# Row tiles of a quantised layer spread over four half steps, projections beside them, on one Trainium2 core

## Chip, cores, metric

One core of a Trainium2 chip. The time is device microseconds of one execution of the whole program. TensorE, VectorE, ScalarE, GpSimd and SyncE (which only issues DMAs here) each run their own instruction stream and meet at semaphores. In the profile's rows they are PE (weight loads: PEld), DVE, ACT, POOL and SP.

## What is computed

Four images of 512 tokens by 256 go through five layers, each (but the first) followed by a layer norm over the residual sum. Cut to what matters:

```
h = tok(x)                          # relu(x W0) * (x W1) -> Wo
h = norm(h + attn0(h))              # 16 heads of 16, window of +-64 keys
h = norm(h + ffn0(h))               # 8-bit activations, ternary weights
h = norm(h + attn1(h))              # causal
h = norm(h + moe(h))                # 8 experts, top 2

def act_quant(x):                   # per row
    scale = 127 / max(|x|)
    return clip(round(x * scale), -128, 127) / scale
g, u = bitlinear(x, w_gate), bitlinear(x, w_up)      # 256 -> 1024
h = relu(g) ** 2 * u
ffn0 = bitlinear(h, w_down)                          # 1024 -> 256
```

## The kernel before

Up to some 700 us the kernel works through attention in half steps (`HALVES`, the numbers `eta`). A unit is one tile of 128 rows for four heads; a half step is two heads of a unit. There are 128 units, so half steps 0 to 255, 32 to an image; image 0 to 3 of the window layer come first, then the same four of the causal layer. In each half step all engines do a fixed list: scores of unit eta/2 on TensorE (L809) and their row maxima on VectorE (`maximum`, L1099); 15 half steps later the turned scores (L832), whose exponent ScalarE takes (L630); every second half step a triangle or band is cut off on GpSimd (`select`, L540 to L548) and, 19 half steps after the scores, the values are multiplied (`values`, L848, with `vaug` as stationary side). Each eight half steps the maxima are split in three bf16 parts, turned and sent as extra rows, and four heads go back to rows.

Between these stand the dense steps. `DENSE` gives for each phase and image the half step of its step 0 and `STEPS` the number of steps; `SCHED` puts step c at half step at + c. Within a half step every engine runs `dense(phase, i, c)` last; TensorE and ScalarE have an `early` part too, before the turned scores. Phases: `tok`; `qkv` (projections; index 0 to 3 window layer, 4 to 7 causal): step 0 turns the rows, steps 1 to 4 each make one part of 128 of the queries or keys (L947), which ScalarE copies twice (L709, L710), and VectorE and GpSimd split in three bf16 parts (L1325, L562, L1320); steps 5, 6 make the values (L956), which ScalarE writes to `vaug` (L718). SyncE then copies the parts to the ring of three blocks `qs`, `ks` (`stack`), where it waits for the last turned scores of the block before in the slot. `o`: output projection, residual, norm. `ffn`: the quantised layer. `gate`, `route`, `send` (L582): the choice of experts and the row scatters from GpSimd.

The quantised layer of image i: steps 0, 1 (`quant`) scale and round the rows, step 3 (`FQT`) turns them behind 12 warm-up matmuls, and the four row tiles follow, tile t at step 3 + 2t (`FIRST_TILE`, `PER_TILE`, `tile_at(c, off)`). For tile t at offset 0 TensorE makes gate and up of the first 512 columns (`quantised_half`, L875), ScalarE takes relu and square of gate (L658, L661), VectorE multiplies with up (`hidden`, L1284) in the same half step; at offset 1 the second 512 columns, then maximum and scale (L1291 to L1300) on VectorE and the scaled rows on ScalarE (L753); at `QUANT` = 2 VectorE rounds (L1307); at `TURN` = 3 TensorE turns behind three warm-up matmuls (L794, L1000) and ScalarE copies (L644); at `DOWN` = 4 the second product (L983) and its sum (L1366); at `STATS` = 5 and `NORM` = 6 the norm.

PSUM: one bank is kept for the values; the other seven go round. `take` gives each use, in the order of TensorE's stream, the bank longest not used, and TensorE waits (`opened`) until the bank's last reader is done. A bank of "up" is read by VectorE in `hidden`. Behind half step 297 come experts and the last norm, which the change does not touch.

Of the kernel before, what the change touches and what calls it, by code (L numbers as in the profile page):

```python
# [7 lines left out]
BF16 = mybir.dt.bfloat16  # L8
# [5 lines left out]
P = 128  # L14
B, S, D = 4, 512, 256
# [39 lines left out]
VW = H * SLOT + 16  # L55
NR = 3
UNITS = 2 * B * NG * NT
TO_ROWS, TO_TURNED, TO_VALUES, TO_BACK, TO_HEADS = 11, 15, 19, 28, 29
# [28 lines left out]
def turned_heads(u, half):  # L87
# [9 lines left out]
    ("tok", 0, -20), ("qkv", 0, -8), ("tok", 1, 0), ("bias", 0, 1), ("bias", 1, 2), ("wq", 0, 4), ("wq", 1, 8),  # L97
    ("wq", 2, 12), ("qkv", 1, 14), ("tok", 2, 22), ("tok", 3, 34), ("qkv", 2, 46), ("o", 0, 54), ("ffn", 0, 60),
    ("qkv", 3, 77), ("o", 1, 85), ("ffn", 1, 91), ("qkv", 4, 108), ("o", 2, 117), ("ffn", 2, 123), ("qkv", 5, 140),
    ("o", 3, 149), ("ffn", 3, 155), ("qkv", 6, 172), ("o", 4, 181), ("gate", 0, 185), ("route", 0, 187), ("send", 0, 196), ("qkv", 7, 204), ("o", 5, 213),  # L100
    ("gate", 1, 217), ("route", 1, 219), ("send", 1, 228), ("o", 6, 245), ("gate", 2, 249), ("route", 2, 251), ("send", 2, 271), ("o", 7, 278), ("gate", 3, 282), ("route", 3, 284), ("send", 3, 293))
STEPS = {"tok": 12, "qkv": 8, "o": 6, "ffn": 16, "gate": 2, "route": 9, "send": 4, "bias": 2, "wq": 4}


FQT, FIRST_TILE, PER_TILE = 3, 3, 2
QUANT, TURN, DOWN, STATS, NORM = 2, 3, 4, 5, 6

# [36 lines left out]


SCHED = {}
for _phase, _i, _at in DENSE:
    for _c in range(STEPS[_phase]):
        SCHED.setdefault(_at + _c, []).append((_phase, _i, _c))
HALVES = range(min(SCHED), max(max(SCHED), 2 * UNITS + TO_HEADS) + 1)  # L150

# [47 lines left out]
def build(nc, xT, w01, wtok, wattn, wo, battn, bvcol, brow, wq0, wdn, wgate, consts, masks, w1, w2, b1, b2, lnrow, out):  # L199
# [3 lines left out]
    with ctx:  # L203
# [118 lines left out]
        with ExitStack() as c2:  # L322
# [99 lines left out]
            with nc.Block() as block:  # L422
# [95 lines left out]
                def _(pool):  # L518
# [10 lines left out]
                    pool.wait_ge(prep_pool, 6)  # L529
                    for i in range(2):  # L530
                        pool.memset(vaug[:, i, :, 0:H * SLOT].rearrange("p t (h s) -> p t h s", s=SLOT)
                                    [:, :, :, DH:DH + 1], 1.0).then_inc(prep_pool, 1)
# [69 lines left out]
                def _(act):  # L602
# [67 lines left out]
                    def dense(phase, i, c):  # L670
# [19 lines left out]
                        if phase == "qkv":  # L690
# [21 lines left out]
                            if c in (5, 6):  # L712
                                k = c - 5
                                key = ("qkv", i, f"v{k}")
                                act.wait_ge(*d_full(key))
                                if i < 2:
                                    act.wait_ge(prep_pool, 8)
                                act.activation(  # L718
                                    vaug[:, i % 2, 2 * k:2 * k + 2, 0:H * SLOT].rearrange(
                                        "p t (h s) -> p t h s", s=SLOT)[:, :, :, 0:DH],  # L720
                                    dense_bank(key).rearrange("p (t h s) -> p t h s", t=2, s=DH),
                                    ACT.Copy).then_inc(d_out(key)[0], 1)
# [14 lines left out]
                        if phase == "ffn":  # L737
# [36 lines left out]
                def _(pe):  # L774
# [61 lines left out]
                    def values(u):  # L836
# [9 lines left out]
                        for j in range(HG):  # L846
                            hd = g % NG * HG + j
                            ins = mm(bank(V_BANK)[32 * j:32 * j + 32, lo:hi],  # L848
                                     vaug[:, s % 2, kt, hd * SLOT:hd * SLOT + 32], p[:, j, :],
                                     start=(kt == 0), stop=(kt == NT - 1), skip_group_check=True,  # L850
                                     tile_position=(0, 32 * j))
# [219 lines left out]
                def _(dve):  # L1071
# [15 lines left out]
                    def maximum(u, half, split):  # L1087
# [7 lines left out]
                        n = 0  # L1095
                        for i, heads in enumerate(score_heads(u, half)):
                            dve.wait_ge(*s_full((u, half, i)))
                            for a, j in enumerate(heads):
                                ins = dve.tensor_tensor_reduce(  # L1099
                                    out=junk[:, AT["s", (u, half, i)][0], a * (hi - lo):(a + 1) * (hi - lo)],  # L1100
                                    in0=score_bank((u, half, i))[:, a * (hi - lo):(a + 1) * (hi - lo)], in1=mask,
# [207 lines left out]
                    def dense(phase, i, c):  # L1309
# [43 lines left out]
                        if phase == "ffn":  # L1353
# [9 lines left out]
                            if t is not None:  # L1363
# [393 lines left out]
```

## Time and profile before

| | us |
|---|---|
| median of 3 runs | 1079.14 (1068.04 to 1080.44) |
| profiled execution | 1079.0 |
| its span, first to last instruction | 1077.1 |
| mean granted TensorE clock | 0.926 of full |

The span is what the profile's rows add up to. "Granted clock" is the share of the full 2.4 GHz that TensorE was given in a stretch.

### The profile page before, as it was taken

The page shows a single profiled execution, that of the slowest core. Times are in us where ns is not written, and L with a number is a line of the kernel's source. Part 1 is how long each engine was busy: PE and PEld are TensorE (multiplying, and loading weights), DVE is VectorE, ACT ScalarE, POOL GpSimd, SP SyncE. Part 2 cuts the span into 40 slices and gives each one's busy share as a digit, 9 for nine tenths or more (in the row PEclk, how much of TensorE's full clock was granted, in tenths as well). Part 3 has the DMA queues.
Part 4 walks back from the last instruction along what each step waited for, and adds up shares of the span by engine and source line. Part 5 has one row for each costly group of instructions (what it writes and reads, how often), then busy time and mean ns, then how long its engine had stood idle before and what let it go on. Part 6 is the DMA issues. An engine that isn't in the chain of part 4 may idle for free. (4 is left out here: it accounts for less than half of the span.)

```text
span 1077.1 us, 14453 instructions
## 1 busy us (share of the span) xinstructions
PE 914.4 (85%) x5031; PEld 561.6 (52%) x5054; DVE 546.3 (51%) x2104; ACT 417.6 (39%) x717; POOL 295.2 (27%) x364
## 2 busy tenths in 40 slices
PE   6897999878879879888987979867999999999940
PEld 3454455534535534434533525344687777777830
DVE  1257434678778678757785767541021112111137
ACT  1315334476475566565635545501311211121003
POOL 5101322413413413301324342335021122112232
PEclk9998999999989999988988988978999999999975
DMA  9882341542253252430564360153142353243242
GB/s 352 146 186 31 32 80 21 60 40 35 27 60 38 32 52 36 48 38 2 60 88 72 38 104 21 57 196 97 40 96 52 118 132 66 77 123 69 25 102 78
DMA packets 57511, 81.49 MB, mean 76 GB/s; under 512 B 6624, under 2 KB 51041, under 8 KB 55008
## 3 DMA queue, kind: packets, MB, share of 16 engines
q1 hardware_dynamic: 49520, 70.48, 32.9%
q0 software_dynamic: 7296, 9.47, 5.2%
q8 instruction: 40, 0.66, 0.3%
q10 hardware_dynamic: 624, 0.63, 0.2%
q14 instruction: 31, 0.25, 0.1%
HBM read 35.37 MB, written 19.68 MB: 51 GB/s over the span
## 5 line engine op out<-in xcount | busy, mean ns | idle before, releaser
L1099 DVE CUSTOM_DVE_ANT_0 junk<-ps,maskb 128x256 bf16<-128x256 f32 (+4 forms) x512 | 206.3, 434 | 96.6 <-PE ps L809 93.2
L630 ACT ACTIVATE probs<-ps 128x512 f32<-128x512 f32 (+1 forms) x304 | 159.2, 550 | 118.5 <-PE ps L832 115.4
L1551 PE MATMUL ps<-dxT,qs 128*128 128x320 f32 x512 | 139.6, 433 | 1.3 <-DVE dxT L1617 1.3
L1563 PE MATMUL ps<-ks,hTe 128*128 128x256 f32 x640 | 139.3, 379 | 0.0
L1587 ACT ACTIVATE hTe<-ps,qs 128x640 f32<-128x640 f32 x64 | 50.8, 794 | 204.6 <-PE ps L1551 204.6
L1563 PEld LDWEIGHTS ps<-ks,hTe 128*128 128x128 f32 x640 | 121.3, 190 | 16.1
L1507 POOL DMA_INDIRECT mixed_rows<-ysb,ids x40 | 61.7, 1543 | 228.8 <-DVE ysb L1637 225.9
L832 PE MATMUL ps<-qs,ks 99*128 99x256 bf16 (+4 forms) x512 | 104.1, 289 | 23.4 <-DVE nmax L1099 13.7
L1551 PEld LDWEIGHTS ps<-dxT,qs 128*128 128x128 f32 x512 | 97.2, 190 | 41.5 <-DVE dxT L1617 1.7
L809 PE MATMUL ps<-ks,qs 96*128 96x256 bf16 (+4 forms) x512 | 106.2, 290 | 11.1 <-DVE nmax L1099 5.4
L848 PE MATMUL ps<-probs,vaug 128*32 128x256 f32 (+4 forms) x1024 | 92.2, 434 | 10.5 <-issue 5.7
L545 POOL TENSOR_SCALAR_AFFINE_SELECT probs<-probs 128x256 f32<-128x256 f32 (+1 forms) x64 | 39.8, 622 | 217.9 <-ACT probs L630 217.8
L809 PEld LDWEIGHTS ps<-ks,qs 96*128 96x128 bf16 x512 | 45.6, 101 | 89.9 <-issue 59.1
L1617 DVE COPY dxT<-ps 128x256 f32<-128x256 f32 x40 | 15.6, 420 | 137.7 <-PE ps L1538 137.7
L540 POOL TENSOR_SCALAR_AFFINE_SELECT probs<-probs 128x512 f32<-128x512 f32 x64 | 40.6, 639 | 154.4 <-ACT probs L630 154.0
L1634 DVE TENSOR_TENSOR ysb<-ps,ks 128x256 f32<-128x256 f32 x40 | 17.0, 424 | 123.4 <-PE ps L1563 123.4
L794 PE MATMUL ps<-maskb,identb 128*128 128x512 bf16 x190 | 62.8, 486 | 11.9 <-DVE posu L1254 4.2
L832 PEld LDWEIGHTS ps<-qs,ks 99*128 99x128 bf16 x512 | 43.7, 100 | 53.5 <-DVE nmax L1099 20.0
L901 PE MATMUL ps<-x_sb,tokw 128*128 128x512 f32 x128 | 64.3, 636 | 7.2 <-DMA tokw<-w 7.2
L947 PE MATMUL ps<-actT,aw 128*128 128x512 f32 x128 | 63.1, 620 | 2.5 <-ACT actT L649 1.6
L794 PEld LDWEIGHTS ps<-maskb,identb 128*128 128x128 bf16 x206 | 22.6, 118 | 47.4 <-issue 26.0
L875 PE MATMUL ps<-qgu,work 128*128 128x512 bf16 x122 | 34.5, 396 | 11.4 <-DVE att L1141 4.0
(183 smaller groups left out, 1242.3 us busy)
## 6 DMA issues: line engine op xcount, KB each, us to landing
qs<-parts SPq DMA_DIRECT2D x96, 128.0 KB, 4.7
ks<-parts SPq DMA_DIRECT2D x96, 128.0 KB, 7.4
qs<-w SPq DMA_DIRECT2D x8, 1024.0 KB
ks<-w SPq DMA_DIRECT2D x8, 1024.0 KB, 4.9
dispatched_rows<-att SPq DMA_DIRECT2D x8, 650.0 KB, 16.9
ks<-dispatched_rows SPq DMA_DIRECT2D x4, 650.0 KB, 7.4
x_sb<-xT SPq DMA_DIRECT2D x8, 256.0 KB, 4.2
mixed_rows<-h SPq DMA_DIRECT2D x4, 512.0 KB
```

The source lines that it names most:

```text
L630: act.activation(probs_of(u)[:, heads[0]:heads[-1] + 1, :], turned_bank((u, half, i))[:, 0:len(heads) * w].rearrange("p (j n) -> p j n", n=w),
L794: mm(o, identb[:, :], maskb[:, 0:S], start=True, stop=True)
L809: ins = mm(o[:, a * (hi - lo):(a + 1) * (hi - lo)], qs[0:KS, r, hd, t * P:(t + 1) * P], ks[0:KS, r, hd, lo:hi], start=True, stop=True)
L832: ins = mm(o[:, a * (hi - lo):(a + 1) * (hi - lo)], ks[0:KM, r, hd, kt * P:(kt + 1) * P], qs[0:KM, r, hd, lo:hi], start=True, stop=True)
L848: ins = mm(bank(V_BANK)[32 * j:32 * j + 32, lo:hi], vaug[:, s % 2, kt, hd * SLOT:hd * SLOT + 32], p[:, j, :], start=(kt == 0), stop=(kt == ...
L901: ins = mm(o, tokw[:, k, col:col + P], x_sb[:, k, :], start=(k == 0), stop=(k == KD - 1))
L947: ins = mm(o, w[:, k, col:col + P], actT[:, k, :], start=(k == 0), stop=(k == KD - 1))
L1099: ins = dve.tensor_tensor_reduce(out=junk[:, AT["s", (u, half, i)][0], a * (hi - lo):(a + 1) * (hi - lo)], in0=score_bank((u, half, i))[:, ...
L1507: pool.indirect_dma_start(out=acc, out_offset=bass.IndirectOffsetOnAxis(ap=ids[:, e, t:t + 1], axis=0), in_=ysb[:, e % 2, t, :], in_offset ...
L1551: ins = mm(bank(2 * (n % 2) + c)[:, 0:HC], w1s[:, e % 2, k, m * P:(m + 1) * P], dxT[:, e % 2, k, c * HC:(c + 1) * HC], start=(k == 0), sto ...
L1563: ins = mm(bank(4 + n % 2)[:, 0:D], hTe[:, e % 2, m, t * P:(t + 1) * P], w2s[:, e % 2, m, :], start=(m == 0), stop=(m == MH - 1))
L1587: act.activation(hTe[:, e % 2, m, :].rearrange("p (a n) -> p a n", a=2), ps[:, 2 * (n % 2):2 * (n % 2) + 2, 0:HC], ACT.Silu, bias=b1s[:, e ...
```

## The change

The quantised layer takes 25 steps instead of 16: a row tile starts every four half steps, and its later parts lie at 4, 6, 7, 8 and 9 instead of 2 to 6. `HIDDEN` = 1 moves both products on VectorE, with maximum and scale, and ScalarE's scaled rows, one half step behind the matmuls and squares that feed them. The projections of images 2 to 7 start earlier (46 to 38, 77 to 66, 108 to 98, 140 to 130, 172 to 162, 204 to 196) and take two half steps a step (`stretched`), so they lie beside the quantised layer of the image before (image 2's beside the last `tok`). Image 2's values would then be written while those of image 0 are read: `vaug` gets a third buffer, with a wait on the values' matmuls from image 3 on. The scratch `junk` of the maxima gives up the slot of the bank that scores never use, to make room.

```diff
-    ("qkv", 3, 77), ("o", 1, 85), ("ffn", 1, 91), ("qkv", 4, 108), ("o", 2, 117), ("ffn", 2, 123), ("qkv", 5, 140),
+    ("qkv", 3, 66), ("o", 1, 85), ("ffn", 1, 91), ("qkv", 4, 98), ("o", 2, 117), ("ffn", 2, 123), ("qkv", 5, 130),
...
-FQT, FIRST_TILE, PER_TILE = 3, 3, 2
-QUANT, TURN, DOWN, STATS, NORM = 2, 3, 4, 5, 6
+FQT, FIRST_TILE, PER_TILE = 3, 3, 4
+HIDDEN = 1
+QUANT, TURN, DOWN, STATS, NORM = 4, 6, 7, 8, 9
...
+def stretched(phase, i, c):
+
+    return 2 * c if phase == 'qkv' and 2 <= i else c
...
-        SCHED.setdefault(_at + _c, []).append((_phase, _i, _c))
+        SCHED.setdefault(_at + stretched(_phase, _i, _c), []).append((_phase, _i, _c))
...
-            vaug = sb2("vaug", [P, 2, NT, VW])
+            vaug = sb2("vaug", [P, NV, NT, VW])
...
-            junk = sb2("junk", [P, BANKS, S], BF16)
+            junk = sb2("junk", [P, BANKS - 1, S], BF16)
...
-                                if i < 2:
-                                    act.wait_ge(prep_pool, 8)
+                                if i < NV:
+                                    act.wait_ge(prep_pool, 6 + NV)
+                                elif k == 0:
+                                    act.wait_ge(pv_mm, NG * NT * (i - NV + 1))
...
-                            t = tile_at(c, 1)
+                            t = tile_at(c, HIDDEN + 1)
                             if t is not None:
                                 act.wait_ge(fh_scaled, NT * i + t + 1)
...
-                            t = tile_at(c, 0)
+                            t = tile_at(c, HIDDEN)
                             if t is not None:
                                 hidden(i, t, 0)
...
-                            t = tile_at(c, 1)
+                            t = tile_at(c, HIDDEN + 1)
                             if t is not None:
                                 hidden(i, t, 1)
                                 hidden_scale(i, t)
```

TensorE in the second image's quantised layer, before, from one tile's warm-up matmuls to the next tile's (`qgu` are the gate and up weights, `qdn` the down weights, `ks,qs` the scores, `qs,ks` the turned ones):

```order
L794 MATMUL ps<-maskb,identb 128x512 x3
L1000 MATMUL ps<-identb,work 128x128 x8
L809 MATMUL ps<-ks,qs 128x256 x2
L832 MATMUL ps<-qs,ks 128x256 x2
L858 MATMUL ps<-cst,oT 128x128 x4
L983 MATMUL ps<-qdn,work 128x256 x8
L875 MATMUL ps<-qgu,work 128x512 x4
L809 MATMUL ps<-ks,qs 128x256 x2
L875 MATMUL ps<-qgu,work 128x512 x4
L832 MATMUL ps<-qs,ks 128x192 x2
L848 MATMUL ps<-probs,vaug 32x256 x4
L794 MATMUL ps<-maskb,identb 128x512 x3
```

All of a tile's work stands between two half steps of attention. After the change (lines are 11 higher), from one gate and up pair on:

```order
L886 MATMUL ps<-qgu,work 128x512 x4
L958 MATMUL ps<-actT,aw 128x512 x2
L820 MATMUL ps<-ks,qs 128x192 x2
L886 MATMUL ps<-qgu,work 128x512 x4
L843 MATMUL ps<-qs,ks 128x192 x2
L859 MATMUL ps<-probs,vaug 32x256 x4
L820 MATMUL ps<-ks,qs 128x192 x2
L843 MATMUL ps<-qs,ks 128x192 x2
L805 MATMUL ps<-maskb,identb 128x512 x3
L1011 MATMUL ps<-identb,work 128x128 x8
L958 MATMUL ps<-actT,aw 128x512 x2
L820 MATMUL ps<-ks,qs 128x192 x2
```

A tile's parts stand in different half steps now, with a projection part (`actT,aw`) in every second.

VectorE at the same place, before, from the rounding of a tile on:

```order
L1307 TENSOR_SCALAR work<-work 128x1024
L1284 TENSOR_TENSOR work<-work,ps 128x512
L1099 ISA junk,nmax<-ps,maskb 128x192
L1099 ISA nmax 128x1
L1126 CAST nparts<-nrest 128x4x4
L1099 ISA junk,nmax<-ps,maskb 128x192
L1099 ISA nmax 128x1
L1129 TENSOR_TENSOR nparts<-nrest,nparts 128x4x4
L1284 TENSOR_TENSOR work<-work,ps 128x512
L1291 TENSOR_REDUCE sm<-work 128x1
```

The rounding is followed at once by the next tile's product, and the second product comes one half step later. After:

```order
L1319 TENSOR_SCALAR work<-work 128x1024
L1160 BN_STATS stat<-att 128x6
L1337 TENSOR_TENSOR proj<-proj,parts 128x512
L1111 ISA junk,nmax<-ps,maskb 128x192
L1111 ISA nmax 128x1
L1111 ISA junk,nmax<-ps,maskb 128x192
L1111 ISA nmax 128x1
L1296 TENSOR_TENSOR work<-work,ps 128x512
```

The product follows a half step of maxima, and a projection's subtraction (L1337) stands between.

GpSimd where the last image's projections stand, before (L582 the row scatters, L540 the selects, L562 the casts of a projection part):

```order
L540 AFFINE_SELECT probs<-probs 128x512
L582 DMA dispatched_rows<-h,posu 5120x260 x4
L540 AFFINE_SELECT probs<-probs 128x4x128 x3
L540 AFFINE_SELECT probs<-probs 128x512
L562 CAST parts<-proj 128x512 x2
L540 AFFINE_SELECT probs<-probs 128x4x128
```

After:

```order
L549 AFFINE_SELECT probs<-probs 128x512
L591 DMA dispatched_rows<-h,posu 5120x260 x4
L549 AFFINE_SELECT probs<-probs 128x4x128
L571 CAST parts<-proj 128x512
L549 AFFINE_SELECT probs<-probs 128x4x128
L571 CAST parts<-proj 128x512
L549 AFFINE_SELECT probs<-probs 128x4x128
```

The casts now follow the scatters after one select instead of four.

## Rows read from the trace of the kernel before

**Rows 1.** Page, part 1: busy us of each engine (share of the span), instructions.
```profile
PE 914.4 (85%) x5031; PEld 561.6 (52%) x5054; DVE 546.3 (51%) x2104; ACT 417.6 (39%) x717; POOL 295.2 (27%) x364
```

**Rows 2.** Busy time by stretch: stretch, length, busy us by engine, granted clock, DMA share, GB/s.
```profile
219.30:246.40 27.10, 20.10 (x156) 10.38 (x158) 20.90 (x65) 19.43 (x31) 4.44 (x8) 1.00 0.23 24
246.40:262.70 16.30, 13.73 (x110) 7.48 (x108) 13.64 (x63) 9.96 (x17) 6.92 (x11) 1.00 0.01 3
279.70:298.70 19.00, 15.17 (x108) 7.92 (x107) 13.98 (x57) 9.46 (x18) 5.51 (x9) 0.91 0.13 23
298.70:329.10 30.40, 23.80 (x166) 12.63 (x166) 23.95 (x79) 19.84 (x31) 5.50 (x9) 0.83 0.40 41
329.10:344.70 15.60, 13.90 (x103) 7.61 (x101) 11.97 (x54) 9.42 (x17) 5.85 (x10) 1.00 0.13 24
344.70:359.40 14.70, 14.60 (x109) 9.84 (x108) 10.25 (x44) 9.59 (x18) 8.99 (x13) 1.00 0.84 85
378.40:409.90 31.50, 23.45 (x166) 11.71 (x166) 25.29 (x80) 19.66 (x31) 5.50 (x9) 0.89 0.38 38
409.90:426.70 16.80, 14.79 (x104) 7.55 (x101) 13.57 (x53) 9.91 (x18) 6.39 (x11) 1.00 0.18 29
564.80:586.90 22.10, 16.68 (x96) 7.41 (x93) 12.28 (x47) 10.52 (x20) 9.95 (x13) 0.85 0.24 63
```

**Rows 3.** The same for the score matmuls (L809) alone, one stretch.
```profile
329.10:344.70 15.60, 2.85 (x16) 1.39 (x17) 1.00 0.13 24
```

**Rows 4.** VectorE in order of time: start, us, instruction, [idle before <-who ended it].
```profile
312.57 0.69 DVE L1284 TENSOR_TENSOR work<-work,ps 128x512 f32<-128x512 f32 x1 [1.14 <-ACT work L661]
313.18 0.42 DVE L1099 CUSTOM_DVE_ANT_0 junk<-ps,maskb 128x256 bf16<-128x256 f32 x1
...
314.26 0.69 DVE L1284 TENSOR_TENSOR work<-work,ps 128x512 f32<-128x512 f32 x1 [0.31 <-ACT work L661]
315.05 1.22 DVE L1291 TENSOR_REDUCE sm<-work 128x1 f32<-128x1024 f32 x1
...
316.86 0.21 DVE L1300 TENSOR_SCALAR sm<-sm 128x1 f32<-128x1 f32 x1
...
318.38 0.69 DVE L1307 TENSOR_SCALAR work<-work 128x1024 bf16<-128x1024 f32 x1 [0.30 <-ACT work L753]
318.99 0.48 DVE L1366 SCALAR_TENSOR_TENSOR att<-ps,sm,h 128x256 f32<-128x256 f32 x1
320.11 0.69 DVE L1284 TENSOR_TENSOR work<-work,ps 128x512 f32<-128x512 f32 x1 [0.64 <-ACT work L661]
```

**Rows 5.** What L1284 waited for in the whole span: us, times.
```profile
  ACT work L661: 26.5, 20
```

**Rows 6.** Fill of the values' buffers on GpSimd, and their first writer on ScalarE.
```profile
15.88 2.02 POOL L528 MEMSET vaug<- 128x2304 f32 x1
...
42.06 0.60 ACT L718 ACTIVATE vaug<-ps 128x512 f32<-128x512 f32 x1
```

**Rows 7.** Groups by shape, 53 to 700 us: count | busy us, mean ns | idle before.
```profile
L947 PE MATMUL ps<-actT,aw 128*128 128x512 f32 x112 | 56.0, 623 | 1.8 <-ACT actT L649 1.6 <-DVE att L1141 0.2
...
L1162 DVE TENSOR_SCALAR h<-att,mv,rstd 128x256 f32<-128x256 f32 x44 | 22.4, 562 | 3.9 <-POOL rstd L555 3.3
L1325 DVE TENSOR_TENSOR proj<-proj,parts 128x512 f32<-128x512 f32 x28 | 19.2, 686 | 1.5 <-ACT parts L710 1.5
...
L865 PE MATMUL ps<-cst,h 128*128 128x128 f32 x56 | 8.5, 297 | 2.3 <-DVE nmax L1099 2.3
```

**Rows 8.** The second subtraction (L1320): duration ns min/median/max.
```profile
L1320 DVE TENSOR_TENSOR parts<-proj,parts x32: 682/690/1747, 37.9 to 593.0; 128x512 bf16<-128x512 f32 x32
```

**Rows 9.** Page, part 6: issues of the stores, KB each, median us to landing.
```profile
ks<-parts SPq DMA_DIRECT2D x96, 128.0 KB, 7.4
```

**Rows 10.** GpSimd and TensorE in order of time, around 573 us.
```profile
572.00 0.97 POOL L582 DMA_INDIRECT dispatched_rows<-h,posu  x1 [0.30 <-issue]
...
573.68 1.94 PE L848 MATMUL ps<-probs,vaug 128*32 128x512 f32 x8 [3.71 <-issue]
```

More of the change, by code:

```diff
@@ L56 @@
 NR = 3
+NV = 3
 UNITS = 2 * B * NG * NT
@@ L97 @@
     ("tok", 0, -20), ("qkv", 0, -8), ("tok", 1, 0), ("bias", 0, 1), ("bias", 1, 2), ("wq", 0, 4), ("wq", 1, 8),
-    ("wq", 2, 12), ("qkv", 1, 14), ("tok", 2, 22), ("tok", 3, 34), ("qkv", 2, 46), ("o", 0, 54), ("ffn", 0, 60),
-    ("qkv", 3, 77), ("o", 1, 85), ("ffn", 1, 91), ("qkv", 4, 108), ("o", 2, 117), ("ffn", 2, 123), ("qkv", 5, 140),
-    ("o", 3, 149), ("ffn", 3, 155), ("qkv", 6, 172), ("o", 4, 181), ("gate", 0, 185), ("route", 0, 187), ("send", 0, 196), ("qkv", 7, 204), ("o", 5, 213),
-    ("gate", 1, 217), ("route", 1, 219), ("send", 1, 228), ("o", 6, 245), ("gate", 2, 249), ("route", 2, 251), ("send", 2, 271), ("o", 7, 278), ("gate", 3, 282), ("route", 3, 284), ("send", 3, 293))
-STEPS = {"tok": 12, "qkv": 8, "o": 6, "ffn": 16, "gate": 2, "route": 9, "send": 4, "bias": 2, "wq": 4}
-FQT, FIRST_TILE, PER_TILE = 3, 3, 2
-QUANT, TURN, DOWN, STATS, NORM = 2, 3, 4, 5, 6
+    ("wq", 2, 12), ("qkv", 1, 14), ("tok", 2, 22), ("tok", 3, 34), ("qkv", 2, 38), ("o", 0, 54), ("ffn", 0, 60),
+    ("qkv", 3, 66), ("o", 1, 85), ("ffn", 1, 91), ("qkv", 4, 98), ("o", 2, 117), ("ffn", 2, 123), ("qkv", 5, 130),
+    ("o", 3, 149), ("ffn", 3, 155), ("qkv", 6, 162), ("o", 4, 181), ("gate", 0, 185), ("route", 0, 187),
+    ("send", 0, 196), ("qkv", 7, 196), ("o", 5, 213), ("gate", 1, 217), ("route", 1, 219), ("send", 1, 228),
+    ("o", 6, 245), ("gate", 2, 249), ("route", 2, 251), ("send", 2, 271), ("o", 7, 278), ("gate", 3, 282),
+    ("route", 3, 284), ("send", 3, 293),)
+STEPS = {"tok": 12, "qkv": 8, "o": 6, "ffn": 25, "gate": 2, "route": 9, "send": 4, "bias": 2, "wq": 4}
+FQT, FIRST_TILE, PER_TILE = 3, 3, 4
+HIDDEN = 1
+QUANT, TURN, DOWN, STATS, NORM = 4, 6, 7, 8, 9
 def tile_at(c, off):
@@ L529, in _ @@
                     pool.wait_ge(prep_pool, 6)
-                    for i in range(2):
+                    for i in range(NV):
                         pool.memset(vaug[:, i, :, 0:H * SLOT].rearrange("p t (h s) -> p t h s", s=SLOT)
@@ L715, in dense @@
                                 act.wait_ge(*d_full(key))
-                                if i < 2:
-                                    act.wait_ge(prep_pool, 8)
+                                if i < NV:
+                                    act.wait_ge(prep_pool, 6 + NV)
+                                elif k == 0:
+                                    act.wait_ge(pv_mm, NG * NT * (i - NV + 1))
                                 act.activation(
-                                    vaug[:, i % 2, 2 * k:2 * k + 2, 0:H * SLOT].rearrange(
+                                    vaug[:, i % NV, 2 * k:2 * k + 2, 0:H * SLOT].rearrange(
                                         "p t (h s) -> p t h s", s=SLOT)[:, :, :, 0:DH],
@@ L848, in values @@
                             ins = mm(bank(V_BANK)[32 * j:32 * j + 32, lo:hi],
-                                     vaug[:, s % 2, kt, hd * SLOT:hd * SLOT + 32], p[:, j, :],
+                                     vaug[:, s % NV, kt, hd * SLOT:hd * SLOT + 32], p[:, j, :],
                                      start=(kt == 0), stop=(kt == NT - 1), skip_group_check=True,
@@ L1096, in maximum @@
                         for i, heads in enumerate(score_heads(u, half)):
+                            b = AT["s", (u, half, i)][0]
                             dve.wait_ge(*s_full((u, half, i)))
@@ L1099, in maximum @@
                                 ins = dve.tensor_tensor_reduce(
-                                    out=junk[:, AT["s", (u, half, i)][0], a * (hi - lo):(a + 1) * (hi - lo)],
+                                    out=junk[:, b - (b > V_BANK), a * (hi - lo):(a + 1) * (hi - lo)],
                                     in0=score_bank((u, half, i))[:, a * (hi - lo):(a + 1) * (hi - lo)], in1=mask,
```

## Prediction

> **What bounds the kernel now.** I read the page's first part first: TensorE is busy 85% of the span, VectorE 51% [rows 1]. An average over stages says little here, so next came the busy time by stretch. The first 700 us are attention, cut into 256 half steps, and each stretch of [rows 2] holds eight of them: [rows 3] counts 16 score matmuls, two a half step. In the period of the second image (half steps 88 to 119, 79.7 us) the stretches take 19.0, 30.4, 15.6 and 14.7 us. The 30.4 are those in which the quantised layer takes a row tile every two half steps: TensorE is busy 23.80 of them at a granted clock of 0.83 and idle 6.6, VectorE is busy 23.95. The same hump is 31.5 us long in the next image and 27.1 in the first. In the two stretches behind it TensorE is idle 1.7 and 0.1 us at full clock: they are bound by TensorE, and VectorE has a quarter to a third of its time free.
>
> The order of time on VectorE shows what the hump waits for [rows 4]: a product (L1284) starts at 312.57 and the one of the next tile at 320.11, so a tile takes 7.5 us. In it VectorE stands 1.14 us, 0.31, 0.30 and 0.64 for ScalarE (squares, L661, and the scaled rows, L753), since the product stands in the half step in which its factors are only made. Over the kernel these waits for squares are 26.5 us in 20 places [rows 5]. Experts and the end (from 700 us on) are not touched.
>
> **The change part by part.** The sum is made against the profiled execution: 1079.0 us, a span of 1077.1 and 1.9 around it; the median of the three runs, 1079.14, is the same.
>
> *No work goes or comes*, but for the third value buffer: one more ones memset and a fill of 3456 instead of 2304 elements on GpSimd, 2.02 us for the 2304 and ended near 18 us, while its first user on ScalarE starts at 42.1 [rows 6]. Cost 0, some 22 us of cover. The scratch tile of the maxima loses a slot nothing used.
>
> *Redistribution.* I price one tile and one projection. On VectorE a tile is two products of 0.69, a reduce of 1.22, four small ones of 0.8 together (from the reduce's end at 316.27 to 317.07), 0.69 to round, 0.48 to add [rows 4], and some 1.0 for the norm (0.56 [rows 7]) and its statistics: 5.5 us. A part of the projections costs TensorE 56.0/28 = 2.0 us (28 parts lie in the rows' stretch, four matmul records each) and VectorE two subtractions of 0.69 each [rows 7, 8]. Written into the half steps of the tables (tile steps at 91 to 115 instead of 91 to 106, projections at 98 to 112 instead of 108 to 115), VectorE's busy time in the four stretches changes by -2.7, -7.5, +11.6 and -1.3 us: from 14.0, 23.9, 12.0, 10.2 to 11.3, 16.4, 23.6, 8.9. The first hands on one product, reduce and small ones (2.7). The second held three tiles' products and reduces, four roundings, three sums and two norms, some 17 us; now it holds two, two, one and none and a first subtraction, some 9.5. The third held 4 us (a last sum and norm, three subtractions) and now holds three products, two reduces, two roundings, two sums, two norms (10.7) and seven subtractions (5). TensorE's changes by 0, -3.7, +6.2 and -2.5 and loses the low clock's share in the hump (0.17 of it, of which I count 2 us): from 15.2, 23.8, 13.9, 14.6 to 15.2, 18.1, 20.1, 12.1.
>
> What a stretch takes beyond the larger load is read from stretches without a tile at work or with two engines loaded: 16.3/13.7 = 1.19, 15.6/13.9 = 1.12, 14.7/14.6 = 1.01 and 16.8/14.8 = 1.14 [rows 2]; I take 1.12 where two are loaded, 1.06 where VectorE alone leads and its squares are ready beforehand. The first stretch (end of the output projection, start of the quantised layer with its chain) only loses the first product's wait: 19.0 - 0.7 = 18.3. Then 18.1 x 1.12 = 20.3; 23.6 x 1.06 = 25.0; 12.1 with 0.5 of idle = 12.6. Together 76.2 against 79.7: -3.5 us an image, -14 for the four images with such a layer. The other images have the same table beside other loads (humps of 27.1 and 31.5 us); I use one figure for all. Bounds of an image: if the 50.3 us of TensorE behind the first stretch ran without a gap, -11; if the coupling of 1.19 held on both crowded stretches, 18.3 + 21.5 + 28.1 + 12.6 = 80.5, +0.8. I stay near the middle because the stretches with both engines loaded lie between 1.12 and 1.19. For four images: -44 to +3.
>
> *The products half a step later* belong to it: the waits of [rows 5] go (they are most of the 6.6 us idle of the hump, so they are within the sum, not beside it). What is late next is PSUM: a bank of "up" results is held a half step longer, and seven banks go round. By the bank table three takes an image (turned scores at half step 99, first projection part at 100, values at 108) now want a bank that VectorE frees in the same half step; before there was one. TensorE then waits for a pair of maxima (two of 0.42, overlapping a little) and one product, some 1.45 us, less what it has to do before (0.36 of scores and more): 0 to 1 us each. I take it as inside the 1.12.
>
> *Projections earlier.* Image 2's move beside the last image of the token layer, where TensorE is full either way: 0. The projections' stores wait, on SyncE's queue, for the ring of three blocks: the first block of an image is free one half step after turned scores that stand where they stood, so the stores of image 4 leave at half step 110 (before, from 109) and are wanted at 128. Behind them on the queue stands nothing earlier than the next image's stores. ScalarE's wait for them before it overwrites a part comes at half step 72 at the earliest, ten after their issue at 62: 20 us of cover over a landing of 7.4 us [rows 9]. Cost 0; were the cover gone, ScalarE would stand up to 7 us once an image.
>
> *The last projection, 204 to 196.* In [rows 10] GpSimd works through eight row scatters of 0.97 us with the selects of two units behind them, and TensorE, which needs those selects, stands 3.71 us before L848 and runs on at the low clock (L848 takes 1.94). That stretch is 22.1 us long with 16.7 busy at 0.85. Now the turned rows (8.5/7 = 1.2 us) and the first part (2.0) [rows 7] stand in that place on TensorE and use the wait: -3.2, and -0.8 of clock: -4. Bounds: 0 (the wait moves along with it) and -6.
>
> Sum: -14 - 4 = -18, so 1079 - 18 = 1061 us.
>
> One row speaks against moving subtractions beside more of GpSimd's work. The longest of the 32 subtractions took 1.75 us where the median is 0.69 [rows 8]: something blocked it for a microsecond. What that makes is the fourth rival below. The Trainium skill, "SBUF — State Buffer", on who interferes with whom, says that a VectorE instruction with two SBUF inputs contends with a GpSimd instruction that reads SBUF, and that the later one is fully blocked. The trace agrees in one instruction, and its median says that most escape. By the rule as it stands each moved subtraction can meet a select or a cast, which the sum leaves out.
>
> **The rivals.**
> 1. *The pile-up eats it (no change).* In half step 104 VectorE has the pair of maxima (0.8), a quarter of the split maxima (0.4), product, reduce and small ones (2.7) and two subtractions (1.4): 5.3 us, TensorE some 3.4 (a part of 2.0 and the scores); in 105 VectorE has 1.6. If neither engine runs ahead by more than two half steps, 96 to 111 take the larger load of each pair, 43.3, and with 1.06 on it 45.9: nothing against the 46.0 of now. With the tail -4 or 0: 1075 to 1079, say 1077. For it: the coupling by banks of one or two half steps. Against: the stretch at 246 us (13.7 and 13.6 busy in 16.3).
> 2. *The held banks cost TensorE (slower).* At the three takes VectorE is a half step late because it is the fuller engine there, so TensorE stands 1.45 plus a product and a maximum, 2.7 us, three times in four images: +32, and 1061 + 32 = 1093. It beats the gain once a take costs more than 18/12 = 1.5 us. For it: VectorE is as full as TensorE in the hump already [rows 2]. Against: by my loads it leads only in 104 to 111.
> 3. *Both engines close up fully.* -11 an image and -4: 1031. For it: 14.6 busy of 14.7 at 344.7. Against: there VectorE was loaded by two thirds only.
> 4. *Shared port.* Each of the 32 moved subtractions loses half a select, 0.3 us: +10, so 1071. Against: the median of 0.69 with a minimum of 0.68.
>
> **How the numbers follow.** Forecast 0.45 (its own range 1050 to 1070), no change 0.25, slower 0.12, full closing 0.13, port 0.05. The likeliest gives 1061. The range leaves out the far end of 3 and of 2: 1042 to 1086. About 2% (21.6 us, so below 1057.5) is what a measurement of this kernel tells from no change: all of 3 and a good half of the forecast's lower part, 0.13 + 0.25 = 0.38; slower by over 2% needs takes of over 3 us, half of rival 2: 0.06; the rest 0.56.
>
> **What would show it.** Right: no stretch of eight half steps over 27 us between 200 and 500 us; the L1284 wait for L661 under 8 us; TensorE's clock 0.95 or more where it was 0.83; half steps 96 to 111 near 45 us rather than 46, and 112 to 119 near 12.6; the 3.71 us before L848 under 1.5. Wrong if TensorE stands over 1.5 us for products or maxima at the three takes; if VectorE's idle time goes but the two stretches together stay at 46 us (rival 1); if subtractions have a median over 0.8 us (rival 4); if the first stretch grows past 19 us, since the start of the layer then pays for work moved behind it.

## The result, and the profile after

| | before | after |
|---|---|---|
| median, us | 1079.79 (4 runs) | 1064.66 (4 runs, 1060.62 to 1067.54) |
| ratio | | 0.989 (0.984 to 0.994) |
| span of the profiled execution | 1077.1 | 1061.0 |
| mean granted clock | 0.926 | 0.936 |

The forecast was 1061 in a range of 1042 to 1086. In a second set beside the experiments the changed kernel took 1061.1 (ratio 0.986, 0.983 to 0.989). Against 1077.1 to 1079.8 for before, that is 15 to 16 us less. One execution of the first experiment took 2712 us; the ratio given there leaves it out, and without it that kernel's median is 1087.1.

Busy time by stretch of the changed kernel (stretch, length, busy us by engine, granted clock, DMA share, GB/s). A stretch of eight half steps runs from one score matmul to the sixteenth after it, since two belong to each half step. The four from 282.8 on are half steps 88 to 119 and answer to the 79.7 us of [rows 2]; the first two are half steps 40 to 55; those at 540 and 558 are 192 to 207, the latter's counterpart in [rows 2] being the one of 22.1 us.

```profile
164.20:189.60 25.40, 24.46 (x130) 14.15 (x129) 11.45 (x44) 10.80 (x20) 7.41 (x11) 1.00 0.05 11
189.60:204.70 15.10, 12.02 (x100) 7.97 (x98) 8.73 (x43) 7.46 (x15) 9.03 (x12) 0.92 0.83 89
...
282.80:300.90 18.10, 13.72 (x109) 7.39 (x107) 14.61 (x60) 9.46 (x18) 5.52 (x9) 1.00 0.13 24
300.90:321.20 20.30, 17.05 (x127) 9.04 (x123) 15.31 (x57) 15.36 (x27) 5.66 (x9) 1.00 0.60 60
321.20:342.30 21.10, 19.39 (x146) 11.97 (x142) 19.69 (x65) 15.71 (x27) 8.32 (x13) 1.00 0.05 14
342.30:359.80 17.50, 14.44 (x111) 9.34 (x108) 11.00 (x50) 7.57 (x14) 7.67 (x11) 0.80 0.76 77
...
540.20:558.50 18.30, 15.86 (x101) 6.68 (x98) 15.02 (x73) 8.51 (x18) 5.90 (x7) 0.91 0.91 123
558.50:575.50 17.00, 15.62 (x97) 7.34 (x94) 12.65 (x46) 10.95 (x22) 9.61 (x14) 1.00 0.30 68
```

The hump is gone: 30.4 us became 20.3 at full clock. Its load moved into the next stretch (15.6 to 21.1), and the fourth grew from 14.7 to 17.5 though TensorE has about as many matmuls there (111 records against 109). Together 77.0 instead of 79.7, so 2.7 us for this image. TensorE is idle 3.1 us of the fourth and its clock is 0.80 there, where it was idle 0.1 at 1.00.

The changed kernel was traced once more (beside the second set of experiments). The first three stretches are 18.1, 20.3 and 21.1 us again, but the fourth is this:

```profile
340.50:356.00 15.50, 13.14 (x112) 8.38 (x109) 10.95 (x50) 7.51 (x14) 7.61 (x11) 0.89 0.85 87
```

So of the fourth's growth 0.8 us stands in both traces, with TensorE idle for 2.4 us and more, and 2 us only in the first, at its lower clock. Over the four images the fourth stretches together did not grow: 64.6 us before, 63.2 and 61.2 after.

What TensorE, VectorE and ScalarE waited for over the whole span (us in total, times, longest), changed kernel:

```profile
ACT work L764 <- DVE sm L1312: 17.7, 12, 2.9
...
PE ps L843 <- DMA qs<-nrows: 9.8, 7, 3.1
...
PE ps L843 <- DVE work L1296: 5.8, 6, 1.4
...
DVE work L1296 <- ACT work L670: 3.9, 4, 1.4
...
PE ps L805 <- DVE work L1296: 3.7, 4, 0.9
...
PE ps L820 <- DVE work L1296: 3.5, 5, 1.4
...
PE ps L994 <- ACT work L653: 3.1, 7, 0.8
```

VectorE's wait for squares, 26.5 us in [rows 5], is 3.9. In its place TensorE now waits 5.8 + 3.7 + 3.5 = 13.0 us until a product (L1296) frees a bank, never over 1.4 at once; and the wait for the extra rows' DMA, 5.4 us before, is 9.8 (8.1 in the second trace). Where the fourth stretch loses is seen in TensorE's order of time, at the output projection's first steps:

```profile
352.03 0.70 PE L876 MATMUL ps<-cst,att 128*128 128x128 f32 x4 [1.91 <-DVE att L1153]
...
355.28 0.50 PE L843 MATMUL ps<-qs,ks 99*128 99x192 bf16 x2 [0.73 <-DMA qs<-nrows]
355.72 1.08 PE L859 MATMUL ps<-probs,vaug 128*32 128x256 f32 x8
356.73 3.26 PE L984 MATMUL ps<-awo,actT 128*128 128x256 f32 x8
```

TensorE ran ahead, stood for the heads' rows (L1153, on VectorE behind the layer's last norm), and then worked at the lower clock: eight matmuls that are busy for 27.3/14 = 2.0 us on average before (14 such steps, L973) take 3.26 here. In the second trace the wait of 1.91 us is there again, the one for the DMA is not, and the eight take 1.99. The projections that used to stand in this place are done already.

### The profile page after: what moved, and what is told of

Its sections match the earlier page's. It is cut to its first block and busy times, and to the rows that moved or that the text cites. A ratio compares the mean times of both kernels' runs of the same rounds, so it can differ in the third digit from the quotient of the medians.

```text
span 1061.0 us, 14484 instructions
## 1 busy us (share of the span) xinstructions
PE 906.2 (85%) x5054; PEld 561.3 (53%) x5054; DVE 546.7 (52%) x2104; ACT 416.0 (39%) x717; POOL 303.1 (29%) x365
## 5 line engine op out<-in xcount | busy, mean ns | idle before, releaser
L859 PE MATMUL ps<-probs,vaug 128*32 128x256 f32 (+4 forms) x1024 | 88.9, 420 | 8.1 <-issue 4.6
L1629 DVE COPY dxT<-ps 128x256 f32<-128x256 f32 x40 | 15.6, 419 | 139.6 <-PE ps L1550 139.6
L843 PEld LDWEIGHTS ps<-qs,ks 99*128 99x128 bf16 x512 | 43.3, 99 | 51.8 <-DMA qs<-nrows 12.5
L1111 DVE DVE_READ_ACCUMULATOR2_ANT nmax<- 128x1 f32 x512 | 41.8, 82 | 0.0
```

The source lines that it names most:

```text
L843: ins = mm(o[:, a * (hi - lo):(a + 1) * (hi - lo)], ks[0:KM, r, hd, kt * P:(kt + 1) * P], qs[0:KM, r, hd, lo:hi], start=True, stop=True)
L859: ins = mm(bank(V_BANK)[32 * j:32 * j + 32, lo:hi], vaug[:, s % NV, kt, hd * SLOT:hd * SLOT + 32], p[:, j, :], start=(kt == 0), stop=(kt = ...
L1111: ins = dve.tensor_tensor_reduce(out=junk[:, b - (b > V_BANK), a * (hi - lo):(a + 1) * (hi - lo)], in0=score_bank((u, half, i))[:, a * (hi ...
```

## The experiments

Each is compared with runs of the kernel before on the same chip: 1076.1 in the first set, 1077.1 in the second, 1076.5 in the third. The changed kernel in the second set is the anchor.

**Products back in their step** (changed kernel, all else kept):

```diff
-HIDDEN = 1
+HIDDEN = 0
```

> The changed kernel with HIDDEN = 0: both products, maximum and scale back in the half step of their matmuls, all else as changed. Forecast's theory (the late products are worth it, VectorE no longer stands for squares): the 3.9 us of waits for squares go back towards 26.5, TensorE's 13 us of waits ended by products go to about 2, and as VectorE is the fuller engine the time rises by 4 to 8 us, to some 1070. Rival (a bank held longer costs as much as the wait for squares did): the time stays within 3 us of the changed kernel's 1064.7 or falls by up to 5.

Measured 1088.5, ratio 1.012 (1.008 to 1.015): 22 to 24 us above the changed kernel's 1064.7 and 11 to 12 above before. The direction is the one that my theory gave, the size is three times what I gave. Its waits:

```profile
ACT work L764 <- DVE sm L1312: 42.7, 16, 4.6
...
DVE work L1296 <- ACT work L670: 41.6, 23, 4.2
...
PE ps L994 <- ACT work L653: 24.8, 16, 4.7
```

The waits for squares came back and grew to 41.6 us, and in its order of time ScalarE's two copies of a projection part (L718, L719) stand just ahead of relu and square (L667, L670); that these copies are the reason is argued, not tested. And two rows stand here that I had not thought of: ScalarE stands for the scale (42.7 instead of 17.7), and TensorE for ScalarE's copy of the turned rows (24.8 instead of 3.1). Half steps 104 to 111 take 25.2 us with 21.2 busy. The time is lost in the first two images: their periods of 32 half steps (56 to 87, 88 to 119) take 91.2 and 84.8 us, where the changed kernel takes 78.1 and 77.0; the next two take 83.1 and 84.3 against 81.5 and 83.7. Why these lose so little with the same waits is not shown.

**Tiles and late products without the projections' move** (projections at their old half steps; HIDDEN stays 1, so this is not the spreading of the tiles by itself, which was not run):

```diff
-    return 2 * c if phase == 'qkv' and 2 <= i else c
+    return c
...
-("qkv", 2, 38), ("qkv", 3, 66), ("qkv", 4, 98), ("qkv", 5, 130), ("qkv", 6, 162), ("qkv", 7, 196)
+("qkv", 2, 46), ("qkv", 3, 77), ("qkv", 4, 108), ("qkv", 5, 140), ("qkv", 6, 172), ("qkv", 7, 204)
```

> The tiles at four half steps and the late products, but all projections at their old half steps, one half step a step. Theory of the hole (the projections left TensorE without work before the output projection, half steps 112 to 119 went from 14.7 to 17.5 us): that stretch goes back to 15 us or holds the tail of the crowd, the wait of the first turned output rows for att goes from 14.3 back to about 5 us, and the time is 1062 to 1068 although the last projection is back too (+5). Theory of the pile-up (tiles and projections must not meet at full rate): half steps 104 to 119 take over 42 us and the time is 1072 or more.

Measured 1071.7, ratio 0.996 (0.994 to 0.999), which is 4 us below before and at the pile-up's end. Half steps 88 to 119 of its trace:

```profile
285.30:304.20 18.90, 15.13 (x110) 7.87 (x109) 14.62 (x60) 9.54 (x18) 5.52 (x9) 0.91 0.13 23
304.20:320.20 16.00, 12.67 (x112) 6.54 (x109) 13.55 (x52) 12.00 (x21) 4.90 (x8) 1.00 0.76 75
320.20:343.80 23.60, 20.46 (x142) 11.76 (x139) 18.52 (x70) 15.70 (x27) 6.16 (x10) 0.93 0.09 17
343.80:364.50 20.70, 18.02 (x128) 12.28 (x127) 14.62 (x51) 10.75 (x19) 10.39 (x14) 0.92 0.60 60
```

The hump is only shifted: 16.0 us with TensorE idle 3.3, then 44.3 us for the two crowded stretches. Sum 79.2 against 79.7. The fourth stretch holds the tail of the crowd, which the hole theory allowed, but its other two marks are missed: the time is above 1062 to 1068, and the wait of the turned output rows for `att`, asked to fall from 14.3 to about 5 us (matmuls and weight loads together), is 17.3.

**Projections alone** (moved and stretched, a tile every two half steps, products in their step):

```diff
-STEPS = {"tok": 12, "qkv": 8, "o": 6, "ffn": 25, "gate": 2, "route": 9, "send": 4, "bias": 2, "wq": 4}
+STEPS = {"tok": 12, "qkv": 8, "o": 6, "ffn": 16, "gate": 2, "route": 9, "send": 4, "bias": 2, "wq": 4}
...
-FQT, FIRST_TILE, PER_TILE = 3, 3, 4
-HIDDEN = 1
-QUANT, TURN, DOWN, STATS, NORM = 4, 6, 7, 8, 9
+FQT, FIRST_TILE, PER_TILE = 3, 3, 2
+HIDDEN = 0
+QUANT, TURN, DOWN, STATS, NORM = 2, 3, 4, 5, 6
```

> The projections moved and stretched, third buffer of values, but a tile every two half steps and products as before. If the gain needs the tiles spread: the hump of half steps 96 to 103 grows from 30.4 to 33 us or more since VectorE gets subtractions on top, 104 to 111 falls below 15, holes before the output projection as in the changed kernel; time 1074 to 1084. Rival (the projections' move is what gained, by filling TensorE in the hump): 1066 or less.

Measured 1079.3, ratio 1.002 (1.000 to 1.005): nothing gained. The hump is 32.0 us (24.33 of TensorE, 25.36 of VectorE), the two stretches behind it 16.2 and 13.2, and the sum is 79.5. The time is in the range that I gave; the hump grew less than to the 33 us, and half steps 104 to 111 did not fall below 15. The holes are here too: VectorE waits 27.0 us for the output projection between 200 and 545 us, and the rows' DMA holds TensorE 13.0 us there.

The last two runs together tell apart the two waits in TensorE's order of time above. In matmuls' waits over the whole span, the one for the heads' rows is 0.8 us before, 5.2 in the changed kernel, 6.7 with tiles and late products alone and 0.8 with the projections alone: it follows the tiles. The one for the extra rows' DMA is 5.4, 9.8, 4.8 and 16.9: it follows the projections' move.

**The last projection back** at half step 204:

```diff
-    return 2 * c if phase == 'qkv' and 2 <= i else c
+    return 2 * c if phase == 'qkv' and 2 <= i < 7 else c
...
-("qkv", 7, 196)
+("qkv", 7, 204)
```

> The changed kernel with the last image's projections alone back at half step 204, one half step a step. By the forecast their move gives 4 us (measured in the two traces: half steps 192 to 215 from 55.1 to 49.8 us), so 1069 to 1070, with the wait of 3.7 us before the values after the row scatters back. Rival (the time comes back later, in the next scatters): within 2 us of the changed kernel's 1064.7.

Measured 1068.1, ratio 0.992 (0.989 to 0.995), between 3.4 and 7.0 above the changed kernel's two medians. The move of the last image's projections is worth some 5 us; the traces of before and after say 55.1 against 49.9 us for half steps 192 to 215, and this run's says 55.4. The wait for the select behind the scatters is back too, 3.18 us.

**First product late, alone,** in the table of before:

```diff
-                            t = tile_at(c, 0)
+                            t = tile_at(c, HIDDEN)
                             if t is not None:
                                 hidden(i, t, 0)
```

with HIDDEN = 1, the second product and all else as before (third value buffer and smaller scratch stay in).

> The kernel before (tile every two half steps, projections where they were; third value buffer and smaller scratch stay in), with the first product of a tile alone a half step later, next to the second, which stays. It takes away most of the longer waits for squares. If these waits by themselves set the pace of the hump (26.5 us in it): 6 to 12 us less than before, 1066 or so. If the tile's chain through one buffer of hidden rows sets it (product, product, reduce, scale, round, next product: 7.3 of the 7.5 us): same as before, 1072 to 1080.

Measured 1069.6, ratio 0.993 (0.991 to 0.996): 7.5 us less than before. VectorE's wait for squares is 10.4 us in 18 places instead of 26.5, and the hump of half steps 96 to 103 is 27.9 us. So this wait was on the path, and one line of the change gives half of its gain; with the old spacing of the tiles it does at least as well as the spread tiles with both products late (1071.7, ratio 0.996). Both products late with a tile every two half steps was not tried: by my table of bank uses one of the seven would be wanted by scores before VectorE could free it behind those scores. No run shows this.

**Projections four half steps later** (images 3 to 6; image 2 two later):

```diff
-("qkv", 2, 38), ("qkv", 3, 66), ("qkv", 4, 98), ("qkv", 5, 130), ("qkv", 6, 162)
+("qkv", 2, 40), ("qkv", 3, 70), ("qkv", 4, 102), ("qkv", 5, 134), ("qkv", 6, 166)
```

> The changed kernel with the projections of images 3 to 6 four half steps later (70, 102, 134, 166) and image 2's two later (40), so that they end at the output projection. Theory of the hole: half steps 112 to 119 fall from 17.5 to about 15 us, the wait for the extra rows' DMA (9.8 us) to about half, 104 to 111 stay at 21; 1059 to 1062, against 1064.7 for the changed kernel. Rival: VectorE's subtractions then meet the layer's last norm and the output projection's sums, and what 96 to 111 save comes back in 112 to 120: within 2 us of the changed kernel.

Measured 1055.1, ratio 0.980 (0.976 to 0.983): 6 us below the changed kernel beside it, where I had expected 3 to 6. Once more, as an anchor for the third set:

> The kernel of e6 once more, as the anchor: 1055.1 within 3 us, some 7 to 10 us below the changed kernel.

Measured 1054.8, ratio 0.981 (0.974 to 0.987). Half steps 88 to 119 of that trace:

```profile
279.20:299.40 20.20, 16.42 (x109) 8.23 (x107) 14.62 (x60) 9.47 (x18) 5.52 (x9) 0.83 0.12 21
299.40:316.60 17.20, 13.66 (x119) 7.48 (x115) 14.66 (x56) 13.17 (x24) 4.89 (x8) 1.00 0.72 71
316.60:337.30 20.70, 19.41 (x135) 10.49 (x136) 17.75 (x62) 15.36 (x25) 7.14 (x11) 1.00 0.06 14
337.30:353.50 16.20, 14.68 (x127) 10.65 (x124) 13.65 (x54) 9.54 (x18) 9.81 (x13) 1.00 0.82 83
```

The fourth stretch has more VectorE work than in the changed kernel (13.65 against 11.00) and takes 16.2 us at full clock, between the changed kernel's 15.5 and 17.5. The second, which gave two early parts away, fell from 20.3 to 17.2. Over the four images (half steps 56 to 183) the second stretches fall from 88.3 and 89.1 us in the two traces of the changed kernel to 78.2, the fourth rise from 63.2 and 61.2 to 68.2, and all half steps together go from 320.3 and 320.4 to 315.7. TensorE's idle time in the fourth falls from 8.8 and 8.1 to 4.8 us: the hole was real, and filling it leaves the second stretch lighter. A further 2.8 us (83.5 to 80.7) fall in half steps 24 to 55 and belong to image 2's projections, two half steps later. The wait for the extra rows' DMA is 5.5 us over the span of this trace, as good as the 5.4 before the change.

**No warm-up matmuls at the turns** (the three before each turn of rounded rows left out):

```diff
                                 o = d_open(("ffn", i, f"f{t}"))
-                                keep_busy(o, 3)
```

> The changed kernel without the three warm-up matmuls before each of the 16 turns of rounded rows (48 matmuls, 0.22 to 0.36 us each at full clock). If TensorE is now the bound in the crowded stretches and needs no warming there (granted clock 1.00 in 96 to 111): 8 to 12 us less, 1054. If the clock falls again as in the hump of before (0.83): no gain or up to 5 us more, 1064 to 1070.

Measured 1062.7, ratio 0.987 (0.984 to 0.990), against 1061.1 for the changed kernel beside it. A miss for the first theory: 48 matmuls less give nothing. Half steps 96 to 111 of its trace:

```profile
297.80:319.70 21.90, 19.00 (x124) 10.14 (x121) 15.73 (x57) 15.71 (x27) 5.50 (x9) 0.84 0.56 56
319.70:340.80 21.10, 18.38 (x141) 11.43 (x138) 19.71 (x65) 15.61 (x27) 8.37 (x13) 1.00 0.06 14
```

In the first of them the clock fell to 0.84 and 20.3 us became 21.9, as the second theory had it. But elsewhere it rose (half steps 56 to 71: 0.97 and 1.00 against 0.81 and 0.92), and over half steps 56 to 183 it is 0.945, against 0.950 and 0.945 in the two traces of the changed kernel. Over those half steps work turned into waiting: TensorE is busy 264.7 us instead of 273.4 and 274.9, and idle 53.8 instead of 46.9 and 45.5. Half steps 104 to 111 take 21.1 us as before with 1.0 us less of TensorE's work. The rows' DMA holds TensorE 12.3 us over the span instead of 9.8 and 8.1.

**The changed kernel again:**

> The changed kernel once more, as the anchor for the three beside it: 1064.7 within 3 us, a ratio to before of 0.984 to 0.994.

1061.1, ratio 0.986 (0.983 to 0.989).

**Second product back in its step,** the first late:

```diff
-                            t = tile_at(c, HIDDEN + 1)
+                            t = tile_at(c, 1)
```

at both places, that of VectorE (second product, maximum, scale) and that of ScalarE (scaled rows).

> The changed kernel with the first product late (its step as changed) but the second product, maximum, scale and ScalarE's scaled rows back in the half step of the second squares. If e1 lost 24 us because square, product, reduce, scale and scaled rows (some 5.2 us) were squeezed into one half step of 2.6 us, so that ScalarE's next copy and the second product's matmuls came late: most of that loss is here too, 1076 or more, with TensorE's wait of L994 for L653 above 10 us. If it was the first product's wait for its squares that blocked VectorE: within 4 us of the changed kernel, 1061 to 1068.

Measured 1073.4, ratio 0.998 (0.995 to 1.001): 12 us above the changed kernel, so half of the first experiment's loss. That is below the 1076 I had asked for and above the 1068 of the other theory; TensorE's wait of L994 is above the 10 us. Its waits:

```profile
ACT work L764 <- DVE sm L1312: 39.1, 16, 2.6
...
PE ps L994 <- ACT work L653: 19.4, 16, 3.5
...
DVE work L1296 <- ACT work L670: 13.1, 17, 1.6
```

All 16 tiles show it: ScalarE stands at the scaled rows (L764) for the scale, TensorE at the second product's matmuls (L994) for ScalarE's copy (L653). In the changed kernel the copy is issued ahead of the scaled rows of the same half step; here it stands behind those of the half step before. The time is again lost in the first two images alone (89.0 and 82.2 us; the next two take 79.7 and 83.9). In half steps 72 to 79, 30.2 us instead of 21.7, TensorE is idle 6.0 instead of 1.2 and its clock is 0.83 instead of 1.00: the chain's waits and the lower clock share the loss.

**Projections six half steps later:**

```diff
-("qkv", 3, 70), ("qkv", 4, 102), ("qkv", 5, 134), ("qkv", 6, 166)
+("qkv", 3, 72), ("qkv", 4, 104), ("qkv", 5, 136), ("qkv", 6, 168)
```

> As e6 (1055.1), the projections of images 3 to 6 another two half steps later (72, 104, 136, 168), so that their last part lies in the output projection's first steps. If the hole before the output projection is still worth filling: 1052 to 1055. If e6 has it filled and the parts now meet the output projection on VectorE: 1055 to 1060.

Measured 1050.9, ratio 0.978 (0.972 to 0.984), 3.9 below its anchor and a little below the 1052 to 1055 that I gave if the hole was still worth filling. Half steps 56 to 183 take 313.1 us. The fourth stretch is full now:

```profile
334.50:351.00 16.50, 16.41 (x131) 11.36 (x128) 13.54 (x55) 10.68 (x20) 11.09 (x15) 1.00 0.81 82
```

**Four later, and the last image's at 198:**

```diff
-("qkv", 7, 196)
+("qkv", 7, 198)
```

> As e6, the last image's projections at 198 instead of 196. If the place beside the row scatters needs the first part no earlier: 1054 to 1056, no difference; if the wait behind the scatters comes back (3.7 us before the values, low clock after it): 1058 to 1060.

Measured 1049.2, ratio 0.976 (0.969 to 0.982), the fastest of all: 5.6 below its anchor. I expected no difference or a loss. Half steps 192 to 215 in its trace take 48.8 us, in the anchor's 51.9:

```profile
529.80:547.00 17.20, 15.22 (x97) 6.26 (x94) 14.20 (x71) 7.82 (x16) 4.49 (x6) 0.80 0.84 111
547.00:564.00 17.00, 15.40 (x92) 6.57 (x88) 12.16 (x46) 10.39 (x21) 10.85 (x14) 1.00 0.33 80
564.00:578.60 14.60, 14.60 (x108) 9.23 (x105) 10.61 (x43) 9.69 (x20) 5.64 (x7) 1.00 0.79 78
```

```profile
532.50:551.40 18.90, 16.93 (x101) 7.00 (x98) 15.04 (x73) 8.32 (x17) 5.92 (x7) 0.82 0.80 112
551.40:568.30 16.90, 15.55 (x96) 7.29 (x92) 12.74 (x46) 10.86 (x22) 9.54 (x14) 1.00 0.30 68
568.30:584.40 16.10, 14.57 (x101) 8.62 (x98) 9.47 (x41) 8.54 (x17) 5.00 (x6) 0.90 0.73 71
```

The parts now reach into the stretch before the output projection, where TensorE was idle 1.5 us at a clock of 0.90 and now has no gap. That seems to account for 3.1 of the 5.6 us, but the other trace of the anchor's kernel takes 14.4 us for this stretch at full clock, and 50.2 for all three: so 1.4 to 3.1. What both traces show is the first of the three, 17.2 us against 18.9 and 18.8. A further 2.6 us between the two traces lie before half step 24, where the two programs are the same; what this says of the medians is open.

## Why the prediction was right, and where not

*What bounded the kernel.* Right: the hump of a tile every two half steps, with TensorE and VectorE each busy for under four fifths of it and VectorE standing for squares. The wait of [rows 5] was on the path: with 16 of its 26.5 us gone the time fell by 7.5 us.

*The redistribution, -14.* The total came out: the four periods of half steps 56 to 183 are 79.0, 79.7, 83.8 and 89.1 us before and 78.1, 77.0, 81.5 and 83.7 after, so -0.9, -2.7, -2.3 and -5.4, together -11. Of these TensorE's idle time gives 4.9 (51.8 to 46.9) and its busy time 6.4 (279.8 to 273.4) for the same work, at a mean clock of 0.950 instead of 0.933. By stretch, two terms were off and cancelled. The second was forecast at 20.3 and is 20.3, the first at 18.3 and is 18.1, both partly by luck: the second has 17.05 us of TensorE at a coupling of 1.19, not 18.1 at 1.12, and the first has VectorE's load unchanged (14.6, not 11.3) but a clock of 1.00 instead of 0.91; over the four images the first did not fall (79.4 before, 79.9 and 81.3 after) and the second is 22.2 on average. The third was forecast at 25.0, from 23.6 us of VectorE, and is 21.1 with 19.7 busy: I had put 4 us too much into it, which VectorE did in the first and the fourth. The fourth was forecast at 12.6 and is 17.5 and 15.5 in the two traces (15.8 and 15.3 on average over the images): the step that failed is "12.1 with 0.5 of idle", where TensorE is idle 3.1 and 2.4 and, at the lower clock, busy 14.4 and 13.1. I asked what the projections meet where they go, not what TensorE has left where they came from. What showed it was the trace after, and the two later tables: with the projections reaching into this place the whole kernel is 6 to 10 us faster, some 3 of them by image 2's move.

*The products half a step later.* The price of the bank was right: 13.0 us of TensorE's waits end at a product instead of 1.5, each at most 1.4. But I booked the late product as one term among others, inside the hump. It is the condition for the rest: with tiles and projections spread as in the change but products in their step, the kernel is 12 us slower than before; tiles with late products gain 4 and projections alone nothing. The mechanism I left out is the chain squeezed in one half step: square, product, reduce, scale, scaled rows. It makes ScalarE stand, and its next copy hold TensorE. Moving the second product alone is worth 12 us in the changed table, the first another 12 to 15.

*Projections earlier, 0.* Off by 2 us. Half steps 32 to 55 went from 60.0 to 62.0: the extra rows leave at half step 52 and are wanted at 55, and with the projections gone from there TensorE stands 3.1 us for the landing instead of 2.3, at a clock of 0.92 over half steps 48 to 55 instead of 1.00. With image 2's projections two half steps later, half steps 32 to 55 take 59.2. I had looked at the stores' waits alone.

*The last projection, -4.* Right: 5.2 us by the two traces, 3.4 to 7.0 by taking it back. The 3.71 us before the values of [rows 10] are gone. The same wait behind the next image's scatters, 3.7 us in half step 235, stays; no projections are left to put there. Half steps 216 to 255, which the change does not touch, take 69.2 us in both traces of the changed kernel and 72.3 before; in the other runs they take between 69.8 and 73.3, with and without the moved projections, so these 3 us are of no known cause.

*Third buffer, stores, shared port: 0.* Nothing in the trace speaks against it. The 32 second subtractions have a median of 0.682 us and a longest of 1.131, against 0.690 and 1.747 in [rows 8]. The rule of the Trainium skill ("SBUF — State Buffer", who interferes with whom) would have made the fourth rival; the trace does not show it at work beyond single instructions. Of the 64 subtractions of both kinds six take 0.78 us or more, where one did before; each of the six overlaps a select on GpSimd, and together they are 1.9 us over the median, not the 10 of the rival.

*The rivals.* The pile-up as I wrote it (no gain in 96 to 111) is false: 41.4 us against 46.0. The held banks cost what they cost, about 1 us a wait, and not the 2.7 that would have turned the sign. The full closing did not come, and the two later tables show that part of it was to be had: 73.5 us for the period at 1050.9.

*The signs.* No stretch over 27 us, squares under 8 us, the 3.71 us gone and the clock at 1.00 in the hump came as written. Half steps 96 to 111 are 41.4 us, further down than the "near 45". "112 to 119 near 12.6" did not come.

## What to carry to other kernels

When work moves to fill a gap, look at the place it leaves as closely as at the place it goes to: there it may have covered a DMA or another engine's in-order queue. Here shifting it by four to six steps gave 6 to 10 us, about what the projections' move had given (7 to 11, from 1071.7 to 1064.7 and 1061.1). Where a chain of four or five operations crosses engines inside one slot of a hand-written order, give each link its own slot before spreading or interleaving anything. Spread first and the chain can get longer, since each engine now has more to do between two links. Test the parts of a combined change both alone and left out: here spread tiles with late products gave 4 us, moved projections 0, both moves without the late products lost 12, and all three together gave 15.

## What the runs showed of the hardware

The same instructions do not always get the same clock. In the traces of two programs that are alike up to half step 196 (four later, and the same with the last image at 198), half steps 0 to 7 took 22.8 us at a mean granted clock of 0.87 in one and 21.3 at 0.93 in the other; half step 24 began at 121.3 and at 118.7 us. That 2.6 us is of the size of the spread between runs of one kernel, and as large as an image's gain here. A difference of two single traces of that size, in a stretch with unequal clocks, is no proof by itself. Of the readings above the fourth stretch of the changed kernel is such a case (17.5 us at 0.80, 15.5 at 0.89, one program). Half steps 88 to 95 are not, though they look like it: 18.1 us at 1.00 in both traces of the changed kernel, and 20.2 to 20.4 at 0.83 in all four traces with the projections later. The sum over half steps 56 to 183 is steadier than its parts: 320.3 and 320.4 us for the changed kernel, 315.6 and 315.7 for the one four half steps later.

Leaving out 48 matmuls that do no useful work gave no time (1062.7 against 1061.1), although TensorE is 92% busy in the crowded stretch (19.39 of 21.10 us). A busy TensorE was not by itself the bound: it waits in turn for banks, rows and copies, and the warm-up matmuls stand mostly in that time: 9 to 10 us less of busy time over half steps 56 to 183 became 7 to 8 us more of idle time.
